# The last group's depthwise and tail stages in parts of one, one and two images, and state copies at the end of a tail step

## The reference

```
x = x + L0(gn(x))   # focal modulation: 3 depthwise convolutions, gates, layer norm
x = x + L1(gn(x))   # gated MLP with rows quantised to fp8
x = x + L2(gn(x))   # 7x7 circular depthwise filters -> gates -> 8-step log-space scan -> h @ W_out + b_out
x = x + L3(gn(x))   # deformable 3x3 convolution: offsets from a 3x3 convolution,
                    # then 9 positions per pixel, each a bilinear mix of 4 corners, then 9*64 -> 64
```

## Time and profile before

| what | value |
|---|---|
| median of 3 runs | 5637.39 us |
| the profiled execution: its own time, and its span | 5645.93 us, 5644.2 us |
| GpSimd busy | 2868.9 us (51%) |
| VectorE busy | 3302.4 us (59%) |
| TensorE matmul busy | 3107.0 us (55%) |
| ScalarE busy | 1771.1 us (31%) |
| mean granted TensorE clock | 0.668 |

### The profile page before, as it was taken

One profiled execution on the slowest core, in us unless ns is written; L12 is line 12 of the kernel. 1 busy time (PEld: TensorE's weight loads), 2 busy tenths in 40 slices (PEclk: granted clock), 3 DMA queues, 4 the chain that ended last, 5 costly groups with the idle time before them and its releaser, 6 DMA issues. The chain is left out here.

```text
span 5644.2 us, 93453 instructions
## 1 busy us (share of the span) xinstructions
PE 3107.0 (55%) x39702; PEld 2672.4 (47%) x39702; DVE 3302.4 (59%) x4067; ACT 1771.1 (31%) x3401; POOL 2868.9 (51%) x2617
## 2 busy tenths in 40 slices
PE   4872334658844466658745466558744454354332
PEld 3861234557733355547633365448633353344222
DVE  5257833464678755564678755574678745454333
ACT  2123424521234235521234234531234224142000
POOL 1000000464556655564556665564556756677776
PEclk9965655668766665668766666668767666566555
DMA  3941084559833585549833585559843565754333
GB/s 57 177 77 26 24 139 129 142 116 206 166 96 100 121 193 162 132 114 218 163 95 102 127 186 163 140 122 220 159 112 92 121 179 134 180 170 129 112 105 93
DMA packets 773569, 747.77 MB, mean 132 GB/s; under 512 B 575121, under 2 KB 652337, under 8 KB 768721
## 3 DMA queue, kind: packets, MB, share of 16 engines
q1 hardware_dynamic: 648737, 401.89, 34.5%
q0 software_dynamic: 124416, 339.90, 21.5%
HBM read 621.76 MB, written 121.38 MB: 132 GB/s over the span
## 5 line engine op out<-in xcount | busy, mean ns | idle before, releaser
L2099 POOL DMA_INDIRECT e_gb<-corner_table,e_idx x2592 | 2853.7, 1101 | 2755.2 <-DMA e_cws<-cw_all 1131.2
L2161 DVE TENSOR_TENSOR e_vw<-e_gb,e_pc 128x1024 f32<-128x1024 f32 x576 | 776.1, 1376 | 685.4 <-DMA e_gb<-corner_table,e_idx 649.5
L2127 PE MATMUL e_pv<-shifts,e_vw 128*128 128x128 f32 x2744 | 545.5, 369 | 470.9 <-DVE e_vw L2168 470.9
L2127 PEld LDWEIGHTS e_pv<-shifts,e_vw 128*128 128x128 f32 x2744 | 449.0, 193 | 504.4 <-DVE e_vw L2168 482.0
L497 PE MATMUL e_pw<-wk,e_vt 128*64 128x64 f32 (+1 forms) x2880 | 330.7, 289 | 345.8 <-DVE e_xr L2179 220.1
L497 PEld LDWEIGHTS e_pw<-wk,e_vt 128*64 128x64 f32 (+1 forms) x2880 | 285.0, 196 | 419.3 <-issue 261.3
L2137 ACT ACTIVATE e_vt<-e_pv 128x512 f32<-128x512 f32 x288 | 184.8, 642 | 727.8 <-PE e_pw L2127 727.0
L511 PE MATMUL b_p<-b_x,b_tt 100*100 100x96 f32 x4096 | 388.1, 255 | 10.6 <-DMA b_tt<-zl 10.6
L511 PEld LDWEIGHTS b_p<-b_x,b_tt 100*100 100x100 f32 x4096 | 382.0, 173 | 14.0 <-DMA b_tt<-zl 11.8
L1908 ACT ACTIVATE f_xall<-f_p 64x384 f32<-64x384 f32 (+2 forms) x320 | 301.7, 1056 | 120.9 <-PE f_p L1804 118.6
L2168 DVE TENSOR_TENSOR e_vw<-e_vw 128x1152 f32<-128x1152 f32 x233 | 330.2, 1417 | 8.0
(11 more groups left out here) (320 smaller groups left out, 7250.9 us busy)
## 6 DMA issues: line engine op xcount, KB each, us to landing
b_tt<-zl SPq DMA_DIRECT2D x256, 234.0 KB, 8.6
b_tt<-zl SPq DMA_DIRECT2D x128, 390.0 KB, 10.2
e_gb<-corner_table,e_idx POOLq DMA_INDIRECT x2592
d_px<-x_halo SPq DMA_DIRECT2D x32, 1152.0 KB
corner_table<-f_xn SPq DMA_DIRECT2D x128, 288.0 KB
f_xall<-xpad SPq DMA_DIRECT2D x10, 2400.0 KB
x_halo<-d_xo SPq DMA_DIRECT2D x128, 144.0 KB
d_wd<-wd_rows SPq DMA_DIRECT2D x8, 1890.0 KB, 31.6
```

The source lines that it names most:

```text
L2099: nc.gpsimd.indirect_dma_start(self.gb[k][:, 4 * q:4 * q + 4, :].rearrange("p a c -> p (a c)"), None, T.table[m], off)\
L2127: last = nc.tensor.matmul(dst, vw[:, a, 2 * q:2 * q + nq, :].rearrange("p k c -> p (k c)"), T.ident[:, :], start=(a == 0), stop=(a == n - ...
L2161: v.tensor_tensor(dst, self.gb[k][:, 4 * k0:4 * k1, :].rearrange("p (k a) c -> p k a c", a=4), bc(w, [128, k1 - k0, 4, C], 3), ALU.mult).t ...
```

## The change

The last group is done in three parts, of 1, 1 and 2 images:

```
-PARTS = parts_of([(NI,)] * (NGRP - 1) + [(2, 2)])
+PARTS = parts_of([(NI,)] * (NGRP - 1) + [(1, 1, 2)])
```

A part of one image has its own list of weights in F, and D's code guards the second image. A part now counts how often each of the two input buffers has been loaded before it (`seen`), in place of `P.base // 2`:

```
     def steps(n):                       # StageF
+        if n == 1:
+            return [10, 14, 6] + [12, 16, 6] + [12, 10, 8] + [1]
         return [10, 14, 6] + [16, 22, 6] + [22, 26, 6] * (n - 2) + [16, 20, 6] + [12, 10, 8] + [1]
...
             self.st.enter(sp, P.G, P.stage)         # StageD.sp
-            load_x(1)
+            if P.n > 1:
+                load_x(1)
...
-        if k < 2 and p == 0:                        # StageD: sums, squares, normalising
+        if k < min(2, P.n) and p == 0:
```

In all groups, F's state copies for image j+1 are moved from the start of its own step to the end of step j. On TensorE the turns stand after group norm's sum, on ScalarE the copies after the square root and before the wait for the normalised image, and on VectorE the corners after the normalised image and before the positions of image j-2. `taps` then is no longer interleaved with them:

```
         if p == 0:                                  # StageF.pe
-            for g in range(8):
-                if new:
-                    h_turn(g)
-                if old and g >= 1:
-                    taps(0, g - 1, g)
             if old:
-                taps(0, 7, 9)
+                taps(0, 0, 9)
...
             if new:
                 gn.pe_sum(pe, self.psn, NH, gn.of(P, P.n, a))
+            if a + 1 < P.n:
+                for g in range(8):
+                    h_turn(a + 1, g)
...
         if p == 2 and new:                          # StageF.act
             gn.act_std(act, NH, gn.of(P, P.n, a))
+            if a + 1 < P.n:
+                h_moves(a + 1)
             act.wait_ge(S.f_xn, P.base + a + 1)
...
             dve.wait_ge(S.f_xn, P.base + j + 1)     # StageF.dve
+            if j + 1 < P.n:
+                self.corners(dve, P, j + 1)
```

More of the change, by code:

```diff
@@ L1507, in pe @@
             if p == 0:
-                pe.wait_ge(self.p_in[m % 2], 48 * (P.base // 2 + m // 2 + 1))
+                pe.wait_ge(self.p_in[m % 2], 48 * (P.seen[m % 2] + m // 2 + 1))
             conv(2 * p)
@@ L1540, in square @@
         def square():
-            act.wait_ge(self.x_in[k % 2], 64 * (P.base // 2 + k // 2 + 1))
+            act.wait_ge(self.x_in[k % 2], 64 * (P.seen[k % 2] + k // 2 + 1))
             if m >= 1:
@@ L1553, in act @@
             self.st.enter(act, P.G, P.stage)
-        if k < 2 and p == 0:
+        if k < min(2, P.n) and p == 0:
             square()
@@ L1603, in sums @@
         def sums():
-            dve.wait_ge(self.x_in[k % 2], 64 * (P.base // 2 + k // 2 + 1))
+            dve.wait_ge(self.x_in[k % 2], 64 * (P.seen[k % 2] + k // 2 + 1))
             gn.dve_sums(dve, NH, xs[:, 3:NR + 3, :], self.sq, gn.of(P, 0, k))
@@ L1754, in sp @@
             self.st.enter(sp, P.G, P.stage + 1)
-            load(0)
-            load(1)
+            for m in range(min(2, P.n)):
+                load(m)
             for u in range(2):
@@ L1788, in pe, with h_turn @@
         a, b, c = j, j - 1, j - 2
-        def h_turn(g):
-            upto(pe, S.f_ta_free, 14 * P.base + self.turn_h(a) + g - 1)
+        def h_turn(m, g):
+            upto(pe, S.f_ta_free, 14 * P.base + self.turn_h(m) + g - 1)
             for i in range(3):
-                last = nc.tensor.transpose(self.pth[g % 2][:, i, :, :].rearrange("p a b -> p (a b)"), T.H[:, P.first + a, :, 3 * g + i], ident)
+                last = nc.tensor.transpose(self.pth[g % 2][:, i, :, :].rearrange("p a b -> p (a b)"), T.H[:, P.first + m, :, 3 * g + i], ident)
             last.then_inc(S.f_ta_full, 1)
@@ L1844, in pe @@
         new, mid, old = a < P.n, 0 <= b < P.n, 0 <= c < P.n
+        if k == 0:
+            for g in range(8):
+                h_turn(0, g)
         if p == 0:
-            for g in range(8):
-                if new:
-                    h_turn(g)
-                if old and g >= 1:
-                    taps(0, g - 1, g)
             if old:
-                taps(0, 7, 9)
+                taps(0, 0, 9)
             if mid:
@@ L1920, in moves, with h_moves @@
             last.then_inc(S.f_ta_free, 1)
+        def h_moves(m):
+            if m:
+                act.wait_ge(S.f_m_full, 3 * (P.base + m))
+            for g in range(8):
+                act.wait_ge(S.f_ta_full, 14 * P.base + self.turn_h(m) + g + 1)
+                base = (PR - 1 - g // 2) * W + PC - 1 - 3 * (g % 2)
+                hd = self.ht[0:C, :]
+                dst = apv(hd, base, [list(hd.ap[0]), [-1, 3], [PR * W, BR], [PC, BC_]])
+                nc.scalar.activation(dst, self.pth[g % 2], ACT.Copy, bias=1e-6 * 255.0 / 256.0, scale=255.0 / 256.0).then_inc(S.f_ta_free, 1)
         if k == 0:
@@ L1924, in act @@
         new, mid, old = a < P.n, 0 <= b < P.n, 0 <= c < P.n
+        if k == 0:
+            h_moves(0)
         if p == 0:
             if new:
[L1927 to L1936, removed]
+                between()
             if old:
@@ L1977, in dve @@
             v.memset(self.ht[C:C + 2, :], 1.0).then_inc(S.f_one, 1)
[L1978 to L1984, removed]
+        if k == 0:
+            self.corners(dve, P, 0)
         if p == 1 and j < P.n:
-            dve.wait_ge(self.x_in[j % 2], 16 * (P.base // 2 + j // 2 + 1))
+            dve.wait_ge(self.x_in[j % 2], 16 * (P.seen[j % 2] + j // 2 + 1))
             for g in range(3):
@@ L2007, in dve, with corners @@
             self.st.leave(dve)
+    def corners(self, dve, P, m):
+        T, S, v = self.T, self.S, self.nc.vector
+        dve.wait_ge(S.f_ta_free, 14 * P.base + self.turn_h(m) + 8)
+        hd, zz = self.ht[0:C, :], T.zz[:, 96 * (P.first + m):96 * (P.first + m) + 96].rearrange("c (a r b w) -> c a r b w", a=2, r=PR, b=2)
+        for a in range(2):
+            at = apv(hd, a * (H - PR) * W, [list(hd.ap[0]), [W, PR], [W - PC, 2], [1, PC]])
+            last = v.tensor_tensor(at, at, zz[:, a, :, :, :], ALU.mult)
+        last.then_inc(S.f_zz, 1)
     def places(self, dve, link, P, m):
@@ L2179, in result @@
         v.tensor_tensor(xr, xr, self.pso, ALU.add).then_inc(S.e_res, 1)
-Part = namedtuple("Part", "G first n base turn stage")
+Part = namedtuple("Part", "G first n base turn stage seen")
 def parts_of(sizes):
-    parts, turn = [], 0
+    parts, turn, seen = [], 0, (0, 0)
     for G, group in enumerate(sizes):
@@ L2190, in parts_of @@
         for n in group:
-            parts_of_group.append(Part(G, first, n, G * NI + first, turn, 4 + 2 * len(parts_of_group)))
-            first, turn = first + n, turn + 1
+            parts_of_group.append(Part(G, first, n, G * NI + first, turn, 4 + 2 * len(parts_of_group), seen))
+            first, turn, seen = first + n, turn + 1, (seen[0] + (n + 1) // 2, seen[1] + n // 2)
         parts.append(parts_of_group)
     return parts
-PARTS = parts_of([(NI,)] * (NGRP - 1) + [(2, 2)])
+PARTS = parts_of([(NI,)] * (NGRP - 1) + [(1, 1, 2)])
 def sequence():
```

## The result

The changed kernel took 5680.39 us, the median of 4 runs (5661.92 to 5685.22), beside 5639.38 us (4 runs, 5634.34 to 5641.4) for the kernel before: a ratio of 1.0068, 95% interval 1.0044 to 1.0092. Its profiled execution is the fastest of the four: 5661.92 us, with a span of 5660.1.

The account below looks back on a forecast made before the run. No engine is full: stages set the time until the last group, gathers from image 12's first gather on. Terms -73 + 26 + 72 - 10 + 23 + 5 = +43 us on 5637.4 gave 5680 us, range 5635 to 5728.

Parts of the forecast that it names:

- the lead of 43.7 us at image 14: Before the change, image 14's positions begin 43.7 us before its first gather is due; the change was to spend this.
- Rival A: Each image's positions are ready before its predecessor's last gather, so no stops before images 13 and 14: 5582 us, chance 0.12.
- Rival B: No difference: state copies give 59 us in six steps, D and F of image 12 11 us more: 5637 us, chance 0.12.
- Rival C: Much slower: image 12 starts only 40 us earlier, tile-side stage work costs its upper end: 5740 us, chance 0.08.
- Term 1: State copies moved ahead in F, groups 0 to 2: 4.5 us a step, six steps, -27 us, bounds 0 and -59.
- Terms 2 to 4: Ahead of image 12's first gather: D alone -43, F alone -13, tiles moved into the stages before +10 us.
- term 4: Tiles of images 8 to 11 closer in the list, about 3 moved into earlier stages: +10 us, bounds 0 and +20.
- Terms 3 and 4: F of image 12 alone, -13 us, and tiles moved into the stages before D and F, +10 us.
- term 2: D of image 12 alone, without image 13: -40 us, and -3 for load and normalising; bounds -25 and -50.
- Term 6: Stop before image 14 from uncovered steps 2 to 8 of F: 4 + 55 + 12, +72 us, bounds 60 and 90.
- Term 7: Stage work beside tiles: image 12 takes 241 us (-10), image 13 243 us (+23), with 22 us each beside D's loads.
- Terms 5 and 8: Stop of 26 us before image 13 from uncovered steps; F's last steps for image 15 beside image 14's tiles, +5 us.

Follow-up runs that it names:

- e5: The changed kernel run again with no edit: 5685.17 us, ratio 1.0086 to the kernel before.
- e3: Changed kernel with the last group in parts of 2, 1 and 1 images, and one ScalarE tile copy kept: 5615.92 us, ratio 0.9979 to the kernel before.
- e4: Changed kernel with tiles of images 12 and 13 spaced up to the next image's placing, one ScalarE tile copy kept: 5617.34 us, ratio 0.9982 to the kernel before.
- e1: Changed kernel with the last group back in parts of two and two images, only the moved state copies left: 5592.7 us, ratio 0.9941 to the kernel before.
- e9: The kernel with the moved state copies alone, same as e1, on another occasion: 5597.1 us, ratio 0.9941 to the kernel before.
- e2: Changed kernel with the state copies back in their old place, parts of 1, 1 and 2 kept: 5704.8 us, ratio 1.0131 to the kernel before.
- e6: Changed kernel with D's weight loads in the last group's second and third part each followed by a memory-to-memory copy of the same bytes: 5688.51 us, ratio 1.0099.
- e8: Kernel with the copies alone, D's halo and weight loads cut to contiguous runs of at most 4 KB: 5541.16 us, ratio 0.9829 to the kernel before.

## Why the prediction was right

The forecast was 5680 us and the measured median is 5680.39. The near hit is partly chance: I had added 43 us, and the two sets of runs give +38 (1.0068) and +48 (1.0086), or +41 by the medians of the first. And errors of the terms cancelled: image 12 started 24 to 42 us earlier than forecast, while the two stops were 16 to 18 us longer in sum and the profile from which I started took 6.6 us more than the median of its kernel. By my own signs, one spoke against the forecast: "if image 12's first gather comes before 4620". It came at 4616.5 in the first profile and at 4635.2 in `e5`. The other sign, a stop under 35 us before image 14, did not come. By the steps, for the two profiled executions of the changed kernel (first, `e5`):

| step | forecast | measured |
|---|---|---|
| 1 to 4: first gather of image 12 | -73 | -115.5, -96.8 |
| 5: stop before image 13 | 26 | 28.8, 30.1 |
| 6: stop before image 14 | 72 | 85.6, 85.6 |
| 7: image 12, first to last gather and one more | 241 | 244.3, 242.3 |
| 7: image 13, the same | 243 | 244.6, 246.4 |
| 8: images 14, 15 and the end | +5 | -0.2, +0.4 |

**The mechanism** was right: the lead of 43.7 us at image 14 was spent, and steps behind the last tile stopped GpSimd. `e3` takes the stops away and `e4` most of the time they cost, both without taking the third part away. Rival A was out by its own point: positions of image 14 at 5206.95, 74 us after the last gather of image 13 in place of 12 us before. Rival B asked for 59 us from the copies' six steps; `e1` has 33 in all. Rival C asked for a start only 40 us earlier; it was 97 or more.

**Term 1**, the copies, was about right. The 6.6 us are one distance on ScalarE, and not all of it arrives. Group 0 tells what does, since nothing was changed ahead of it. From F's first write to the positions of image 0, two moved copies later, it is 100.9 us before (921 to 1021.67) and 90.3 us in `e1` (`e9`: 90.5):

```profile
920.81 1.98 DVE L1977 MEMSET f_ht<- 2x2304 f32 x1 [0.65 <-DVEq L529]
...
923.18 1.98 DVE L1987 MEMSET f_ht<- 2x2304 f32 x1 [0.65 <-DVEq L529]
...
1013.49 0.48 DVE L2032 TENSOR_TENSOR f_pos<-f_p,grid 128x324 f32<-128x324 f32 x1
```

That is 5.2 us a step where I took 4.5, 31 us over six steps. Image 12 starts 34.8 us (`e1`) and 39.0 us (`e9`) earlier with the copies alone.

**Terms 2 to 4** were too small in sum. They forecast -46 for the parts, and `e2`'s profile has -72.8. There the last state product of D's first part is at 4554.03 and F begins at 4574.98, 50.1 us earlier than in the earlier trace rows (forecast 43):

```profile
4554.03 0.61 DVE L1628 TENSOR_TENSOR region<-d_p,region 96x192 f32<-96x192 f32 x2
...
4574.98 1.98 DVE L1980 MEMSET f_ht<- 2x2304 f32 x1 [0.53 <-issue]
...
4647.03 0.50 DVE L2019 TENSOR_TENSOR f_pos<-f_p,grid 128x324 f32<-128x324 f32 x1 [2.64 <-PE f_p L1841]
```

F then needs 72.1 us to the positions, not 95.1: -23, where I took -13. And the +10 for tiles moved forward (term 4) doesn't show: in `e2` VectorE normalises D's first image at 4376, in the kernel before at 4378. Terms 3 and 4 together are most of what was mis-sized, 20 of the 27 us; the other 7 are term 2.

**Term 6** was 14 us too small, and not in its stage part: from variance to positions I took 55 us and it took 56.2 (5150.78 to 5206.95 in the rows of VectorE above), and the 12 us behind it are right (5206.95 to 5219.06). What I had at 4 us is the time from the last gather's start to the end of its weighing. It was 18.4 us (5132.47 to 5150.86), because F's step 1 stands before that tile in the list and VectorE did its residual and sums first:

```profile
5141.51 2.80 DVE L445 TENSOR_REDUCE gn_red<-f_xs 96x64 f32<-96x1536 f32 x1
5144.24 2.71 DVE L447 TENSOR_REDUCE gn_red<-f_sq 96x64 f32<-96x1536 f32 x1
5146.87 2.60 DVE L2177 TENSOR_TENSOR e_vw<-e_gb,e_pc 128x1024 f32<-128x1024 f32 x2
```

**Term 7** had the right sum for a wrong reason. I charged 22 us of each D to its weight loads as bytes that share the DMA engines. `e6` added the same bytes once more and found 1 to 3 us; `e8` kept the bytes, cut the loads into shorter packets and more DMAs, and took 12 us from image 12. So at least 12 of my 22 us hang on how the loads are cut. The 17.66 us stop for D's second input did go from image 12, as forecast, but a stop of 14.81 us behind late gathers came in its place. It lies in the load of weights and halos:

```profile
4695.59 1.49 DVE L2177 TENSOR_TENSOR e_vw<-e_gb,e_pc 128x1280 f32<-128x1280 f32 x1 [30.29 <-DMA e_gb<-corner_table,e_idx]
```

By the rows (18.1 and 47.7 us) a load of 1890 KB was far from the 6.4 us that the fit of the Trainium skill ("DMA: Bandwidth & Descriptors", section "Anatomy of one DMA — SWDGE (gpsimd) path") gives as an estimate. In `e8` DMAs of a quarter of that size land in 8.8 to 15.0 us beside other loads; by the same fit the estimate for 472.5 KB is 3.1 us. The trace is above the Trainium skill's figure in both. The Trainium skill states that fit for DMAs that GpSimd issues, and SyncE issues these with gathers and other loads under way, so neither trace tests it.

**Terms 5 and 8** held: 28.8 and 30.1 for 26, and nothing for 5.

## What to carry to other kernels

Where an engine lives on a stock that the others fill in a fixed order, count the stock against the steps to the next filling before splitting work finer: a split that starts the first batch earlier and leaves the second uncovered loses more than it wins (in `e2`, the parts alone: -73 us at the start, +120 us in stops). A change of two edits should be timed as two: here one gave 33 us and the other took 74. And beside many small gathers, look at how the large loads are cut and not only at their bytes. A single profile can be 20 us off the median, as the first one here: compare the sets of runs before explaining a difference of that size.

## What the runs showed of the hardware that was not expected

In 20 us inside D's loads the two DMA queues passed 204 and 200 packets, with 14.5 and 2.7 KB in a packet on average, so the small gathers got 15% of the bytes. With runs of 4 KB at most, in the 50 us from the first weight load on, the gathers got 3.02 MB in place of 1.98, the loads lost nothing (8.56 MB against 7.62), and the kernel gained 1.12%. That the queues take turns by the packet would explain it, but the counts are alike in some stretches only (667 and 513 in a longer one), and no run varies the packet length alone. Twice the bytes, the added ones from memory to memory and in no more packets altogether, changed nothing that could be measured. Which of the loads, halos or weights, matters more was not tried.
